# Key and value states: one product over both halves of the values, and the two column sets added afterwards

## What is computed

```python
q = relu(proj(Wq)); k = relu(proj(Wk)); v = proj(Wv)     # (b, 32, 1024, 64)
kv = einsum('bhsd,bhse->bhde', k, v)                      # the states, 64 x 64 per head
qkv = einsum('bhsd,bhde->bhse', q, kv)
key_sum = k.sum(axis=2)
normalizer = einsum('bhsd,bhd->bhs', q, key_sum)
out = (qkv / clip(normalizer, 1e-6)) @ Wo + bo
```

## Time and profile before

| | us |
|---|---|
| median of 3 runs | 2007.04 (2003.31 to 2009.59) |
| the profiled execution | 2002.69 |
| its span, first to last instruction | 2000.9 |
| TensorE busy in the span | 1842.2 (92%) |
| VectorE, ScalarE, GpSimd busy | 1191.6, 716.7, 686.3 |
| stage A in the trace | about 37 to 975 |

### The profile page before, as it was taken

One profiled execution on the slowest core, in us unless ns is written; L12 is line 12 of the kernel. 1 busy time (PEld: TensorE's weight loads), 2 busy tenths in 40 slices (PEclk: granted clock), 3 DMA queues, 4 the chain that ended last, 5 costly groups with the idle time before them and its releaser, 6 DMA issues. The chain is left out here.

```text
span 2000.9 us, 25863 instructions
## 1 busy us (share of the span) xinstructions
PE 1842.2 (92%) x8492; PEld 1450.2 (72%) x8492; DVE 1191.6 (60%) x2112; ACT 716.7 (36%) x1369; POOL 686.3 (34%) x697
## 2 busy tenths in 40 slices
PE   8989999999999999998457898989889999999996
PEld 5657888888888888876356676657768778787784
DVE  4557666666666666677853343647465747566664
ACT  2434454445444444433112232355523122213220
POOL 1435121212112222111353555533344445435442
PEclk9999999999999999998758998988999999999998
DMA  6221454435353525421375999610001011101011
GB/s 237 79 71 60 138 159 130 152 95 164 90 189 105 189 82 186 126 85 37 106 258 162 334 267 261 159 52 11 27 27 42 17 32 48 31 5 53 6 53 42
DMA packets 101122, 218.46 MB, mean 109 GB/s; under 512 B 8640, under 2 KB 33232, under 8 KB 99504
## 3 DMA queue, kind: packets, MB, share of 16 engines
q1 hardware_dynamic: 78848, 168.70, 26.0%
q0 software_dynamic: 11584, 28.97, 6.1%
q10 hardware_dynamic: 10608, 19.74, 3.1%
HBM read 126.02 MB, written 91.37 MB: 109 GB/s over the span
## 5 line engine op out<-in xcount | busy, mean ns | idle before, releaser
L744 PE MATMUL bank<-hT,W1b 128*128 128x512 f32 x512 | 208.9, 408 | 14.8 <-DVE hh L1989 14.8
L1743 DVE RECIPROCAL rr<-rr 128x256 f32<-128x256 f32 x128 | 218.8, 1730 | 4.7 <-ACT num L1212 4.7
L744 PE MATMUL bank<-W1a,hT 128*128 128x512 f32 x512 | 209.7, 410 | 3.4 <-DVE hT L1657 3.4
L745 PE MATMUL bank<-hT,W1b 128*128 128x512 f32 x512 | 204.0, 399 | 0.0
L746 PE MATMUL bank<-hT,W1b 128*128 128x512 f32 x512 | 203.6, 398 | 0.0
L746 PE MATMUL bank<-W1a,hT 128*128 128x512 f32 x512 | 202.0, 395 | 0.0
L745 PE MATMUL bank<-W1a,hT 128*128 128x512 f32 x512 | 201.2, 393 | 0.0
L2115 POOL TENSOR_TENSOR x<-x,tmp 128x512 f32<-128x512 f32 x64 | 101.3, 1583 | 272.2 <-DVE tmp L1735 272.2
L1989 DVE TENSOR_TENSOR hh<-hh,bank 128x512 f32<-128x512 f32 x64 | 43.4, 686 | 195.4 <-PE bank L746 166.0
L1762 DVE SCALAR_TENSOR_TENSOR kt<-bank,kt 128x256 fp32r<-128x256 f32 x128 | 50.8, 397 | 173.9 <-ACT vt L1228 173.7
L2053 POOL TENSOR_TENSOR W<-stage,W 128x1024 fp32r<-128x1024 f32 x32 | 76.9, 2404 | 189.5 <-ACT W L1131 187.2
(11 more groups left out here) (274 smaller groups left out, 4644.0 us busy)
## 6 DMA issues: line engine op xcount, KB each, us to landing
hs_d<-bor SPq DMA_DIRECT2D x24, 1548.0 KB, 11.3
ws_d<-W SPq DMA_DIRECT2D x48, 512.0 KB, 6.3
WB<-ws_d SPq DMA_DIRECT2D x8, 3072.0 KB, 17.9
stage<-wa SPq DMA_DIRECT2D x32, 512.0 KB, 5.3
stage<-wbe SPq DMA_DIRECT2D x24, 512.0 KB, 4.2
stage<-wdn SPq DMA_DIRECT2D x24, 512.0 KB, 3.9
mw<-wmod SPq DMA_DIRECT2D x10, 1024.0 KB, 5.0
hg<-hs_d ACTq DMA_DIRECT2D x39, 258.0 KB, 5.7
```

What stands on the lines that cost most here:

```text
L744: pe.matmul(o, lhs(HI), rhs(HI), start=start, stop=False, **kw)
L745: pe.matmul(o, lhs(HI), rhs(LO), start=False, stop=False, **kw)
L1743: dve.reciprocal(rr[:, pair, h], rr[:, pair, h]).then_inc(r_rec, 1)
```

## The change

`accumulate` issues two matmuls for a pair of heads where it issued three. The high half of the keys is multiplied with the values' high and low columns at once, 2 x 130 = 260 columns moving (in SBUF two pieces of 130), into 260 columns of a bank; the low half of the keys is multiplied with the 130 high columns into the first 130. So columns 0 to 129 hold high times high plus low times high, and columns 130 to 259 hold high times low. Each pair has a bank of its own (4 and 5). The two column sets have to be added: ScalarE copies the second set to a new tile `kvs` in SBUF (two instructions, behind the high half of the queries of pair 0), VectorE adds the first set to it (two instructions, `sum_states`, behind the low half of those queries). `kvb`'s high and low halves are then made from `kvs` in SBUF. Two new semaphores order this, `kv_part` and `kv_sum`.

```diff
@@ accumulate (PE)
-                        last = mm3(bank[4][:, pair * VW:(pair + 1) * VW],
-                                   lambda h: kt[:, t % 2, h, pair * P:(pair + 1) * P],
-                                   lambda h: vt[:, t % 2, h, pair, :],
-                                   t == 0 and pair == 0, t == NT - 1, skip_group_check=True)
+                        o, cols = KV[pair], slice(pair * P, (pair + 1) * P)
+                        pe.matmul(o[:, 0:2 * VW], kt[:, t % 2, HI, cols], vt[:, t % 2, :, pair, :],
+                                  start=t == 0, stop=False, skip_group_check=True)
+                        last = pe.matmul(o[:, 0:VW], kt[:, t % 2, LO, cols], vt[:, t % 2, HI, pair, :],
+                                         start=False, stop=t == NT - 1, skip_group_check=True)
@@ step_a (ACT), behind the high half of the queries of pair 0
+                    if pair == 0:
+                        act.wait_ge(kvmm, s * 4 + 4)
+                        if not (first and b == 0):
+                            act.wait_ge(kvb_lo, s)
+                        for i in range(2):
+                            act.activation(kvs[:, i, :], KV[i][:, VW:2 * VW], ACT.Copy).then_inc(kv_part, 1)
...
-                act.wait_ge(kvmm, s * 4 + 4)
+                act.wait_ge(kv_sum, s * 2 + 2)
...
-                    act.activation(kvb[q, HI, :, q], kv[q, :, q], ACT.Copy)
-                    ins = act.activation(kvb[q, HI, :, other], kv[q, :, P:P + 1].to_broadcast([HD, 2, HD]), ACT.Copy)
+                    act.activation(kvb[q, HI, :, q], kvs[q, :, q], ACT.Copy)
+                    ins = act.activation(kvb[q, HI, :, other], kvs[q, :, P:P + 1].to_broadcast([HD, 2, HD]), ACT.Copy)
@@ DVE
+            def sum_states(s):
+
+                for pair in range(2):
+                    dve.wait_ge(kv_part, s * 2 + (pair + 1))
+                    dve.tensor_tensor(kvs[:, pair, :], KV[pair][:, 0:VW], kvs[:, pair, :], ALU.add).then_inc(kv_sum, 1)
@@ step_a (DVE), behind the low half of the queries of pair 0
+                    if pair == 0:
+                        sum_states(s)
...
-                    dve.tensor_tensor(kvb[q, LO, :, q], kv[q, :, q], kvb[q, HI, :, q].bitcast(F32), ALU.subtract)
-                    last = dve.tensor_tensor(kvb[q, LO, :, other], kv[q, :, P:P + 1].to_broadcast([HD, 2, HD]),
+                    dve.tensor_tensor(kvb[q, LO, :, q], kvs[q, :, q], kvb[q, HI, :, q].bitcast(F32), ALU.subtract)
+                    last = dve.tensor_tensor(kvb[q, LO, :, other], kvs[q, :, P:P + 1].to_broadcast([HD, 2, HD]),
                                              kvb[q, HI, :, other].bitcast(F32), ALU.subtract)
```

More of the change, by code:

```diff
@@ L320, in over_a @@
                     a("ot", [P, 2, 2, S], F32R), a("kvb", [P, 2, 2, P], F32R), a("rr", [P, 2, S]),
-                    a("bor", [P, H]), a("colrow", [NB, H]))
+                    a("bor", [P, H]), a("colrow", [NB, H]), a("kvs", [P, 2, VW]))
         def over_ot(a):
@@ L340, in over_d @@
             return (a("hh", [P, 4, S]), a("mx", [P, S]), a("fl", [P, 6, S], BF16), a("ad", [P, 4, 2, S], F32R))
-        ((_, wm), (kt, vt, qt, ot, kvb, rr, bor, colrow), (_, num), h2, (_, yt, gbt), (M_, crow, sqj, yn, _, cmv, cst, csum),
+        ((_, wm), (kt, vt, qt, ot, kvb, rr, bor, colrow, kvs), (_, num), h2, (_, yt, gbt), (M_, crow, sqj, yn, _, cmv, cst, csum),
          (hh, mx, fl, ad)) = shared([over_pro, over_a, over_ot, over_front, over_slots, over_c, over_d])
@@ L397, in build @@
         NN = [(5, 4), (7, 6)]
+        KV = bank[4:6]
         YB = [6, 7, 1, 5, 0, 4]
@@ L440, in build @@
         kvmm = sem("a_kv_accumulated")
+        kv_part = sem("a_kv_part_copied")
+        kv_sum = sem("a_kv_summed")
         kvb_hi = sem("a_kvb_hi")
@@ L1260, in step_a @@
                     ln_out(ln, 0)
-                act.wait_ge(kvmm, s * 4 + 4)
+                act.wait_ge(kv_sum, s * 2 + 2)
                 if first and b == 0:
                     act.wait_ge(aconst, 1)
-                kv = bank[4][:, 0:2 * VW].rearrange("p (a n) -> p a n", a=2)
                 for lo in (0, HD):
                     q, other = slice(lo, lo + HD), slice(HD - lo, P - lo)
-                    act.activation(kvb[q, HI, :, q], kv[q, :, q], ACT.Copy)
-                    ins = act.activation(kvb[q, HI, :, other], kv[q, :, P:P + 1].to_broadcast([HD, 2, HD]), ACT.Copy)
+                    act.activation(kvb[q, HI, :, q], kvs[q, :, q], ACT.Copy)
+                    ins = act.activation(kvb[q, HI, :, other], kvs[q, :, P:P + 1].to_broadcast([HD, 2, HD]), ACT.Copy)
                 ins.then_inc(kvb_hi, 1)
```

## The result

The changed kernel takes 1982.1 us (median of 4 runs, 1980.7 to 1985.48) against 2005.17 us for the kernel before (4 runs, 2000.96 to 2009.59): a ratio of 0.9885 with a 95% interval of 0.9861 to 0.9909, 23 us or 1.2% faster. The profiled execution took 1980.7 us, its span is 1978.9 us against 2000.9, so 22.0 us less.

What follows compares the result with a forecast made beforehand. TensorE was taken to bound stage A. Savings of 21.7 and 2.1 us, less 0.9 and 0.4 for the added passes, made 22.5 us: 1980.2 us from the profiled execution, 1984.5 from the median; range 1977 to 1994.

Steps and rivals of the forecast that it cites:

- The bound: Middle of stage A: TensorE busy for all 108.00 us of a stretch, work on other engines free until TensorE waits.
- The cost of an accumulate: TensorE in stage A: two matmuls of 260 columns and two of 130 cost 0.458 us instead of 0.667, saving 0.209.
- The price by columns: One matmul of 260 columns on TensorE, scaled from 0.233 us for 512 columns: 0.118 us.
- How many count: Stage A: 104 accumulates in 26 steps save 21.7 us, the last two steps of group 7 nothing, group 0 2.1 us.
- Group 0: First group of stage A: 10 of 16 accumulates gain 2.1 us; ScalarE's added copies cost about 0.9 us in three steps.
- What it adds: ScalarE's copies and VectorE's additions: free in the loop, about 0.9 us in group 0, about 0.4 in group 7's last step.
- Rival 3: kvb's low half, reading two SBUF tiles, gets stuck behind GpSimd's splits: 2029 us; chance 0.06 with other such losses.
- The sum: Whole kernel: 21.7 + 2.1 - 0.9 - 0.4 = 22.5 us saved.
- x at 0.13 us: Upper end of the forecast's own range: a 260-column matmul at 0.13 us was said to cost 5 us, giving 1990.
- that nothing changes in stage B: Stage B and what follows start sooner, otherwise the same; no transfer started late by stage A is waited for.
- 1: Each step's tile 1: TensorE waits for VectorE, losing at most 0.209 us per step, 5.4 us, so 1990 us; chance 0.11.
- 2: Accumulate's matmuls: 260 columns take as long as 512, 0.688 us instead of 0.667, no gain, 2011 us; chance 0.07.

Runs made afterwards that it cites:

- e4: Changed kernel with the low half of the keys also multiplied with all 260 columns, so four products of 260; median 1982.44 us, ratio 0.9898 to the kernel before.
- e1: Kernel before with only the products of 260 and 130 columns, in one bank, no added copies or additions, states wrong; median 1975.43 us, ratio 0.9858.
- e2: Changed kernel with the six matmuls of 130 columns put back, added copies and additions kept; median 2008.63 us, ratio 1.0028 to the kernel before.
- e3: Changed kernel with the sums written to PSUM (bank 4) instead of kvs, and kvb made from there; median 1980.44 us, ratio 0.9868 to the kernel before.
- e6: Changed kernel run once more, unaltered, in one job with e7, with a second profile; 1984.40 us, ratio 0.9886 to the kernel before.
- e7: The kernel of e3 run once more, beside the changed kernel; 1976.63 us, ratio 0.9854 to the kernel before.

## Why the prediction was right, and where it wasn't

**The bound** was read right: the loop steps went from 26.66 to 25.8 us, by what TensorE saves.

**The cost of an accumulate**: 0.458 forecast, 0.457 measured. The step that carried it, that a matmul costs the larger of its stream and the next load, is shown by e4. The price by columns, 0.118 us for 260, was 0.120. The estimate by the Trainium skill's formula (TensorE: Matmul & The Clock Gate, Back-to-back issue gap), 0.111 us, is 9 ns under that.

**How many count**: from step 3 to 28 the changed kernel gains 20.80 us in 25 steps, 0.832 each, where 0.836 was forecast; e1, without the added passes, gains 0.851. That 26 steps count and the last two don't is right: e1's lead is 23.60 us at step 29, 23.59 at step 30 and 23.55 at step 31. Group 0 gave 1.51 us; forecast were 2.1 less 0.9. Both terms were too large: e1 has 1.44, which is 7 `accumulate`s of 0.209 us and not 10, and the passes cost the changed kernel nothing in group 0, though they cost e2 0.73.

**What it adds**: the passes add nothing in the loop, as forecast (645.90 us from step 3 to 28 in e3, 645.89 in e1), and the last step takes 50.14 us in e3 and 49.77 in e1, so the additions ahead of the router's positions cost 0.37 us where 0.4 was forecast. The step that failed is in this part. Rival 3 named the right mechanism, that two inputs in SBUF lock VectorE out beside GpSimd, and looked for it only in the loop. There it does occur, as forecast, for the end of a pair of splits. Timelines of the changed kernel:

```profile
590.67 0.49 DVE L1823 TENSOR_TENSOR kvb<-kvs,kvb 64x128 fp32r<-64x128 f32 x1
...
586.05 4.96 POOL L2069 TENSOR_TENSOR W1a<-stage,W1a 128x1024 fp32r<-128x1024 f32 x2 [16.65 <-ACT W1a L1135]
```

0.49 instead of 0.28 us, under 2.5 us of cover; it ends 0.15 us behind the splits. The forecast was a cost of 0. It isn't quite: these steps take up to 0.1 us more, and from step 3 to 28 the changed kernel takes 646.37 us (646.62 in e6), 0.5 to 0.7 more than e3. But at the end of group 7 GpSimd adds 128x512 tiles of 1.29 us into `x` right at that place, and there the tail waits for VectorE already. The lead fell by 3.4 us from step 28 to 31, where the prediction took off 0.4; the three held subtractions are 3.3 us of VectorE's time, and the lower clock of TensorE behind them goes with the rest of the 3.9 us that lie between this kernel and e3. Walking all uses of the two-input subtraction against all of GpSimd's operations, and not only those of the loop, would have found it: before's rows at 962.58 (GpSimd) and 962.62 (the subtraction) overlap too. Before's trace even has the price in this step. Its operation on `tmp` and `row`, both in SBUF, takes 0.69 us alone and 1.28 beside GpSimd's addition:

```profile
964.16 0.69 DVE L1732 TENSOR_TENSOR tmp<-tmp,row 128x512 f32<-128x512 f32 x1
965.49 1.28 DVE L1732 TENSOR_TENSOR tmp<-tmp,row 128x512 f32<-128x512 f32 x1
...
964.93 1.29 POOL L2112 TENSOR_TENSOR x<-x,tmp 128x512 f32<-128x512 f32 x1 [1.06 <-DVE tmp L1732]
```

**The sum**: 22.5 us forecast, 22.0 in the spans and 23.1 in the medians. That is closer than the working deserves. At the hand-over to stage B the lead is 18.5 us. The rest, 3.5 us, came behind it, where nothing is changed: 2.7 of it is the stretch from stage C to D's first tail, which took 155.4 us in before's profile and 152.7 in the changed kernel's, 1.4 came behind that, and 0.7 were lost in stage B. The second profile of the changed kernel took 155.2 us from C to D's first tail; it hands over 18.0 us to stage B and its span is 1982.5 us, 18.4 us under before. So the gain that the traces show for the change is 18 to 18.5 us; that the total came out nearer to 22.5 is luck. Where no subtraction is held the working is borne out: e3 leads by 23.3 us at step 31. The interval of the ratio in the first runs (18 to 28 us) just contains it, that of the second (19 to 27) doesn't, and the medians, 23.1 and 21.0 us, lie above. Before has one trace, of an execution (2002.69 us) that is 2.5 us under the median; what the rest is, is open.

Two steps of the working behind the sum and its range don't hold. By the prediction's own formula, x at 0.13 us costs 114 x 2 x 0.012 = 2.7 us, not 5. And that nothing changes in stage B was taken from DMA's share in the middle of stage A, while DMA is busy for 0.87 of stage B. From its start to C it took 265.6 us in before and 266.3 in the changed kernel, so it held there, but with a larger lead (e1, e3, e7) it took 267.7 to 269.2.

**The rivals**: 1 didn't happen (two waits for `vt`, 0.5 us in all, from 175 to 790 us) but was near; 2 is out by e4; 3 is told above. The range, 1977 to 1994, held the time.

## What to carry to other kernels

Where weight loads follow one another as fast as the engine takes them, a matmul with few moving columns pays for the load, and doubling its columns is nearly free (0.111 us for 130, 0.120 for 260 here): join products that share the stationary operand and add up afterwards on engines with idle time. Before moving an operand of VectorE from PSUM to SBUF, look for GpSimd operations beside every place where it is read, also in first and last iterations; where there are any, write the intermediate result to PSUM, as e3 does. Date the steps in both traces before explaining a total: a sum that comes out right may hide a loss and a stretch that was short by chance.

## What the runs showed of the hardware that was not expected

- One VectorE subtraction of 0.28 us took 1.39 us when it began 0.03 us behind a GpSimd addition of 1.28 us and read two tiles in SBUF; with one of them in PSUM it took 0.27 beside the same addition. The price is the rest of the other's instruction, not a share of the speed: the held subtractions end 0.14 or 0.15 us behind it, whether they began 0.03 us behind its start (967.73) or 0.34 us ahead of its end (590.67). By the Trainium skill's rule (SBUF — State Buffer, Who interferes with whom) the pair of ports that the two engines share is an exclusive lock, and the order of issue decides who blocks; the trace agrees.
- ScalarE takes longer out of SBUF: the four pieces of `kvb`'s high half have medians of 266 and 261 ns from bank 4 in the kernel before, 303 and 292 from `kvs`:

```profile
L1267 ACT ACTIVATE kvb<-bank x64: 253/266/274, 57.9 to 959.3; 64x128 fp32r<-64x128 f32 x64
L1268 ACT ACTIVATE kvb<-bank x64: 257/261/264, 58.1 to 959.5; 64x128 fp32r<-64x128 f32 x64
```

```profile
L1276 ACT ACTIVATE kvb<-kvs x64: 292/303/309, 57.1 to 939.4; 64x128 fp32r<-64x128 f32 x64
L1277 ACT ACTIVATE kvb<-kvs x64: 287/292/299, 57.3 to 939.6; 64x128 fp32r<-64x128 f32 x64
```

- Two executions of the changed kernel differ by 2.5 us in one stretch of 155 us (stage C to D's first tail), while the start of stage B repeats within 0.6 us. The first profile and e6:

```profile
1306.51:1459.16 152.65, 135.51 (x674) 112.54 (x673) 83.53 (x167) 77.68 (x131) 56.81 (x51) 0.91 0.08 23
1307.06:1462.28 155.22, 138.05 (x675) 114.24 (x674) 83.36 (x167) 77.77 (x131) 56.77 (x51) 0.89 0.07 23
```

TensorE's idle time is the same, 17.1 and 17.2 us; the whole difference is busy time with the same matmuls, at a mean granted clock of 0.91 and 0.89. The nine traces of this case fall into two kinds here: 152.3 to 152.8 us at 0.91 or 0.92 (the first profile of the changed kernel, e1, e7), and 154.5 to 155.5 us at 0.89 or 0.90 (the other six). What decides between them, no run here tells.
